# A fused attention and FFN block on one core: units of attention B in pairs, with another order of ACT, PE, DVE and POOL

## The reference, cut to what matters

```python
x = x + attn_a(layernorm(x))   # 16 heads of 64; q softmax over channels, k softmax over tokens,
                               # context = q^T k, out = context v, then w_out and b_out
x = x + ffn(layernorm(x))      # RWKV: token shift by mu_r, mu_k; sigmoid(xr W_r) * (relu(xk W_k)^2 W_v)
x = x + attn_b(layernorm(x))   # 16 heads of 8, rope on q and k,
                               # softmax(q k^T / sqrt(8)) v, then W_O
x = x + ffn(layernorm(x))      # the same weights
```

## Time and profile before

| | us |
|---|---|
| three runs | 1045.62, 1050.62, 1050.64; median 1050.62 |
| the profiled execution, whole | 1045.19 |
| its span (first to last instruction) | 1043.4 |
| busy: PE / ACT / DVE / POOL | 951.9 / 735.1 / 610.4 / 507.7 |
| share of the span | 91% / 70% / 58% / 49% |
| mean granted TensorE clock | 0.971 |
| chain that ended last | PE 72%, ACT 14%, DVE 6%, issue 3% |

### The profile page before, as it was taken

The page is one execution under the profiler, slowest core; times in us unless marked ns, Lnnn a source line. Parts: engine busy times, 40 slices in busy tenths (PEclk is TensorE's granted clock), DMA queues, the critical chain, the costliest instruction groups (busy, mean ns, idle before and its releaser), DMA issues.

```text
span 1043.4 us, 21070 instructions
## 1 busy us (share of the span) xinstructions
PE 951.9 (91%) x8139; PEld 510.9 (49%) x8139; DVE 610.4 (58%) x1475; ACT 735.1 (70%) x772; POOL 507.7 (49%) x344
## 2 busy tenths in 40 slices
PE   5985889999999999999999999999999999597983
PEld 3874534545454555545454545545554544232322
DVE  5776446566573847556573847656574745655233
ACT  4554667877777777878777777878777776375860
POOL 3758163644727292744637382754637271425000
PEclk9999889999999999999999999999999999798995
DMA  6002222324132332324132232324132232223210
GB/s 174 8 31 90 68 97 69 125 58 133 46 107 87 88 97 83 120 72 127 48 113 78 83 97 82 117 71 132 46 110 69 72 111 72 81 66 101 74 34 15
DMA packets 68657, 87.44 MB, mean 84 GB/s; under 512 B 13633, under 2 KB 40130, under 8 KB 68546
## 3 DMA queue, kind: packets, MB, share of 16 engines
q1 hardware_dynamic: 68546, 85.96, 27.4%
HBM read 16.19 MB, written 20.97 MB: 36 GB/s over the span
## 4 chain that ended last, share of the span: by engine, by line
PE 72%; ACT 14%; DVE 6%; issue 3%; SPq 2%; POOL 2%; DMA 1%; ACTq 0%; DVEq 0%
PE PS L1537 19%; PE PS L1351 8%; ACT work L658 8%; PE PS L1493 7%; PE PS L1407 6%; PE PS L1353 6%; PE PS L1352 5%; PE PS L1346 4%; PE PS L1451 3%; ACT work L652 3%; PE PS L1445 3%; PE PS L1428 3%; PE PS L1458 3%; PE PS L1553 2%; PE PS L1420 2%
## 5 line engine op out<-in xcount | busy, mean ns | idle before, releaser
L658 ACT ACTIVATE work<-PS 128x2048 f32<-128x2048 f32 x224 | 420.8, 1878 | 43.0 <-PE PS L1493 39.0
L1537 PE MATMUL PS<-work,v 128*32 128x512 f32 x2048 | 276.1, 611 | 4.6 <-DVE U L1034 4.1
L652 ACT ACTIVATE work<-PS 128x512 f32<-128x512 f32 x256 | 152.3, 598 | 145.1 <-PE PS L1353 142.9
L426 POOL TENSOR_TENSOR rs<-ve,half_neg 128x4 f32<-128x4 f32 x64 | 65.4, 1022 | 358.7 <-DVE ve L878 358.7
L439 POOL TENSOR_TENSOR work<-work,q_rcp 128x1024 f32<-128x1024 f32 x64 | 121.9, 1904 | 122.0 <-DVE q_rcp L930 122.0
L1493 PE MATMUL PS<-q_st,k_st 32*128 32x512 f32 x896 | 114.5, 501 | 19.6 <-DMA q_st<-qk_lo 10.1
L1351 PE MATMUL PS<-wqk,h1h 128*128 128x512 f32 x256 | 123.7, 483 | 2.6 <-issue 2.6
L1352 PE MATMUL PS<-wqk,h1h 128*128 128x512 f32 x256 | 101.9, 398 | 0.0
L1353 PE MATMUL PS<-wqk,h1l 128*128 128x512 f32 x256 | 101.7, 397 | 0.0
L1493 PEld LDWEIGHTS PS<-q_st,k_st 32*128 32x128 f32 x896 | 43.3, 183 | 108.2 <-issue 76.6
L1351 PEld LDWEIGHTS PS<-wqk,h1h 128*128 128x128 f32 x256 | 48.6, 190 | 86.9 <-ACT work L652 31.0
(11 more groups left out here) (159 smaller groups left out, 1611.0 us busy)
## 6 DMA issues: line engine op xcount, KB each, us to landing
qkv_scratch<-qkv_sb SPq DMA_DIRECT2D x16, 768.0 KB, 4.9
rot<-qkv_sb SPq DMA_DIRECT2D x32, 256.0 KB, 3.0
k_st<-qk_hi SPq DMA_DIRECT2D x128, 64.0 KB, 2.1
k_st<-qk_lo SPq DMA_DIRECT2D x128, 64.0 KB, 2.1
q_st<-qk_hi SPq DMA_DIRECT2D x128, 64.0 KB, 2.1
q_st<-qk_lo SPq DMA_DIRECT2D x128, 64.0 KB, 2.1
parted<-U SPq DMA_DIRECT2D x52, 128.0 KB, 2.9
xa<-in_attn_a_x SPq DMA_DIRECT2D x16, 256.0 KB, 2.9
```

The costliest lines, as they stand in the source:

```text
L426: pool.tensor_tensor(rs[:, :], ve[:, :], half_neg[:, :], ALU.pow).then_inc(rstd[n].sem, 1)
L652: act.activation((EQ, EK)[r // 2][c % 2][:, (r % 2) * 512:(r % 2) * 512 + 512], PS[:, bank, :], ACT.Exp)\
L658: act.activation(probs[n % 2], PS[:, 0:4, :], ACT.Exp).then_inc(z["s_exp"].sem, 1)
L1537: mm = pe.matmul(PS[32 * h:32 * h + 32, 6, :], v_flat[p][:, kc, at:at + 32], probs[n % 2][:, h, :], start=(n % 8 == 0), stop=(n % 8 == 7), ...
```

## The change

- **Three probs buffers.** `work_b` is new; `exp_scores(n)` waits for the product with v of unit `n - 3` instead of `n - 2`. `qk_rot` and `r_sb` go to make room.
- **Pairs.** The 16 units become 8 pairs `k`. ACT: `exp_scores(2k)`, `exp_half(2k - 1)`, `exp_scores(2k + 1)`, `exp_half(2k)`; half 15 falls into the next iteration. PE: `scores(2k)`, both `weigh_values` of the pair before, `scores(2k + 1)`, a small piece, `proj_half(2k)`, a small piece, `proj_half(2k + 1)`.
- **Bank 7** takes all of the small pieces in turn that were spread over banks 4 and 7. `r_copy` and `gates_copied` go; `gates` reads PSUM.
- **ACT gives to DVE** `m_copy`, `h1_copy`, two of the three `p_copy`, and the scaling by mu (`scale_mu` on ACT becomes `scale_and_mix` on DVE).
- **`context_narrow`** makes the context in tiles of 32 columns: 32 products instead of 16 in the code (64 for 32 in the trace, where each float32 product is two).
- **POOL, DVE and SP** get new orders. Rope stands right behind `q_hats(a, 0)` (before: behind `ln3_apply`); on DVE `ln1_norm` and the copy of `proj_b(2)` stand behind `q_sums(a, 0)`, and `ln_norm(1)` and `h1_copy` behind `q_sums(a, 1)`.
- Iteration 16 is a paired step without batch `a`; 17 to 19 drain as before, with the transposes of batch 0's attention B moved a little.

```diff
+        work_b = sb("work_b", [P, 2048])
+        probs = [w.rearrange("p (j n) -> p j n", j=4) for w in (work[:, 4096:6144], work[:, 6144:8192], work_b[:, :])]
```

The core of ACT's paired step:

```diff
+            def paired_step(i, p):
...
+                for k in range(8):
+                    exp_scores(z, b, 2 * k)
+                    if k == 0 and E:
+                        exp_half(s, 15, False)
+                    elif k > 0 and A:
+                        exp_half(a, 2 * k - 1, False)
+                    if E and k == 1:
...
+                        p_copy(l, 1)
+                    if k == 2:
+                        t_copy(s)
...
+                    if k == 5:
+                        hold(act, f1["x"], s - 1, 1)
+                        gates(f1, s, 7)
+                    if E and k == 7:
+                        hold(act, f2["x"], e - 1, 1)
+                        gates(f2, e, 7)
+                    exp_scores(z, b, 2 * k + 1)
+                    if A:
+                        exp_half(a, 2 * k, False)
```

PE's new context, and the core of its paired step:

```diff
+            def context_narrow(a, c):
+                hold(pe, q_hat, a, c + 1)
+                for t in range(PAIRS):
+                    for q in range(4):
+                        rows = slice(32 * q, 32 * q + 32)
+                        head = t * P + q // 2 * DA
+                        mm = pe.matmul(PS[rows, 5, t * DA:t * DA + DA], EK[c % 2][:, t * P + 32 * q:t * P + 32 * q + 32],
+                                       EQ[c % 2][:, head:head + DA], start=(c == 0 and t == 0), stop=(c == NC - 1),
+                                       tile_position=(0, 32 * q), skip_group_check=True)
...
+            def paired_step(i, p):
...
+                for k in range(8):
...
+                    scores(z, b, 2 * k)
...
+                    if k == 4 and A:
...
+                        context_narrow(a, 0)
...
+                    if k > 0:
+                        weigh_values(z, b, 2 * k - 2, 1 - p)
+                        weigh_values(z, b, 2 * k - 1, 1 - p)
+                    scores(z, b, 2 * k + 1)
...
+                    if k == 1 and E:
+                        proj_b(l, 2)
...
+                        wv_ctx_wout(s)
+                    if k == 3:
+                        if E:
+                            hold(pe, x1_ok, s)
+                            heads_out(z, e)
+                        if there(a + 1):
...
+                            head_T(a + 1, 7)
...
+                        proj_half(a, p, 2 * k, False)
...
+                    if k == 1:
+                        hold(pe, p_ev, l, 3 if E else 1)
+                        ctx_wout(s)
+                    if k == 2:
+                        attn_out(s, 1 - p)
...
+                    if k == 3:
+                        if there(a + 1):
+                            hold(pe, h1_sb, a + 1)
...
+                        ffn_T(f1, 1, s)
...
+                    if k == 7:
+                        if E:
+                            hold(pe, f2["x"], e, 1)
...
+                        h3_transposes(s)
+                    if A:
+                        proj_half(a, p, 2 * k + 1, False)
```

The places in DVE's paired step that follow the second and the fourth sum of q:

```diff
+                if A:
+                    sums_of(a, 1)
+                ln_norm(1, s, x1, hn1)
+                if there(a + 1):
+                    h1_copy(a + 1, 1 - p)
...
+                if A:
+                    sums_of(a, 3)
+                ln_norm(2, s, x2, h3)
+                if E:
+                    gate_v(f2, e)
```

726 lines of the change are left out of this document (348 added, 378 removed).

## The result

The changed kernel takes 1260.47 us (median of 4, 1259.57 to 1266.74), the kernel before on the same chip 1050.53: ratio 1.2025, 95% interval 1.1973 to 1.2077. The forecast was 1217 with its own bounds of 1180 and 1260, the range with the rivals 1070 to 1285. The profiled execution took 1259.57 us with a span of 1257.8, 214.4 more than the span before.

A forecast was written before the change was run, and what follows sets the result against it. PE bound the kernel, with about 1 us idle an iteration. Waits and clock raise 58.4 us to 73.75, +184 over 12 iterations, less 12 in iteration 16: span 1215, execution 1217; range 1180 to 1260, with rivals 1070 to 1285.

The forecast's parts named there:

- ACT's chain: Each pair's exponentials on ACT: no pair shorter than 6.52 us; 60 us an iteration; as the only bound 1052 us, 8%.
- nothing else late: Condition for ACT's order alone: the eight pairs take 60 us an iteration, 1.6 more than before.
- DVE behind the sum of q: Pairs 1, 3, 7: PE waits for DVE work behind a sum of q; 62.8 us an iteration, 4.4 more than before.
- POOL beside `ln1_norm`: Pair 1: `q_hats` and rope stretch `ln1_norm` to about 6.8 us; `ctx_wout` starts 6.4 us after PE got there.
- The rival of 18%: Rope or `q_hats` falls outside `ln_norm`, so only the sums bind: 62.8 us an iteration, 1087 us; chance 18%.
- The clock: After pair 1's wait PE runs at half clock: `ctx_wout` 2.4 us, the half 1.6, the next scores 0.36 more.
- The rival of 10%: Clock falls behind the waits in pairs 3 and 7 too: about 2.4 us each, 4.8 an iteration, 1275 us; chance 10%.
- Iteration 3 keeps its pattern: Iteration 3, ahead of the steady stretch, was taken as unchanged: 0 us, with the drain +-4.
- Iteration 16: As a paired step without projections it was to take 50 us instead of 62.5: -12 us.
- SP's order: SP's new DMA order, priced at nothing: stacked copies still issued at least one pair ahead of their scores.
- The narrow context: 64 products in four tiles: 1.08 us taken, as columns decide; bounds 1.08 and 2.16, 52 us at the other end.
- Faster by fewer changes between kinds of product: Rival on PE: each pair saves 0.26 us of changes, 3.1 an iteration with the idle us; 996 us, chance 12%.

The follow-up runs named there:

- e10: e9 with one DVE edit: `ln1_norm` right behind its stats, ahead of `c_norm`; 1063.59 us, ratio 1.0132.
- e8: e7 with `T_sb` copied by DVE behind `ln1_norm` instead of by ACT between pair 2's exponentials; 1107.81 us, ratio 1.0554.
- e4: e3 with the second and fourth sums of q moved behind `ln_norm` and the copy or gate after it; 1157.31 us, ratio 1.1039.
- e2: The changed kernel with only rope moved on POOL, back behind `ln3_apply`; 1257.75 us, ratio 1.2003.
- e1: The changed kernel with the third value product's copy to `qkv_sb` ahead of `ln1_norm` on DVE; 1248.42 us, ratio 1.191.
- e5: The changed kernel with 24 filler matmuls of 512 columns on PE ahead of `ctx_wout` in pair 1; 1257.24 us, ratio 1.1972.
- e6: The changed kernel with the earlier wide context (32 products in two tiles) in place of the narrow one; 1266.26 us, ratio 1.2075.
- e7: e4 with both `k_relu` ahead of the stats on DVE and POOL's second square ahead of the third rsqrt; 1124.06 us, ratio 1.0682.
- e9: e8 with rope behind `q_hats(0)` and `add_bias` on POOL, and the two looks at sums behind `add_x1` on DVE; 1118.14 us, ratio 1.0674.
- e3: The changed kernel with both the edit of e1 and rope moved behind `ln3_apply`; 1227.17 us, ratio 1.1711.

## Why the prediction was right, and where not

**ACT's chain.** Right as a mechanism, and in part by luck as a number. The forecast had 60 us an iteration with "nothing else late", and e10, with the long waits on DVE and POOL gone, has 60.1. But the forecast's 60 have `t_copy` on ACT, 8.3 us in pair 2, and e10 has it on DVE and 7.40 there; the other seven pairs are together 1.0 us longer than forecast. `t_copy` cost 0.96 of waiting in pair 2, and e8 gave 0.7 of it back. In iteration 3, pair 6 takes 6.49 (the minimum was put at 6.52). Of what PE idles more in e10 than before, 2.0 us an iteration are for ACT and 0.9 for DVE, and its busy time is 1.1 less: 1.7 us net, 21 in 12 iterations. With 3.4 us up to iteration 4 and 5.2 less in iteration 16 and the drain that makes the 19 us between the two spans (16 in the medians). So ACT's order is the larger part of why e10 is slower, not all of it; that its chain binds in the other pairs is read from these waits, and only `t_copy` was tested by an edit.

**DVE behind the sum of q.** Right: e4 takes the sums away from in front of `ln_norm`, and pairs 3 and 7 fall by 2.2 and 2.9 us. The forecast waits of 2.9 were 2.4. One small reading was off: sum and reciprocal take 1.50 from 515.62 to 517.12, not 1.47.

**POOL beside `ln1_norm`.** Right in place and size, 6.75 us; e2 and e10 show it from both sides (2.66 with `q_hats` alone beside it, and 1.12 with POOL free). The two causes are not separate: e1 alone brings 1.1 us an iteration, e2 alone 0.7, both 3.6, since each alone sends part of the wait elsewhere. The rival of 18%, that POOL doesn't bind, falls.

**The clock.** In pair 1 right (e5: 1.64 us there, forecast 1.76). The rival of 10%, that it falls behind pairs 3 and 7 too, came in part: pair 4 takes 8.24 on average and 7.45 at full clock, pair 7 in iterations 4 to 13 10.77 and 10.06; that is 1.5 us an iteration, not 4.8. In all, PE is busy 718.4 us in iterations 4 to 15 and 674.5 in e10, which does the same work at 1.00: by an estimate from these two, the clock costs 44 us of the 207 there; the rest is 176 us more idle time, less 13 by which PE's work itself is shorter (687.4 before).

**Mis-sized terms of the sum.** Against 1217 it is 43 us more. (1) Iterations 4 to 15: +22.3, by pairs 12 x 0.94 = 11.3 in pair 4 and 12 x 0.67 = 8.0 in pair 7, most of both the clock's (pair 7 waits 3.3 us in iterations 14 and 15 besides), and 12 x 1.07 = 12.8 in pair 6, where `k_relu` stands behind x2's stats, a wait that I had not looked for; less 10.2 in pair 1 (iteration 15 has no `ln1_norm` and takes 8.11), and small ones. So the terms miss in both directions, and that 1260 lies at the upper edge of the forecast's own bounds owes something to that. (2) Iteration 3: +13.5 where I took 0. "Iteration 3 keeps its pattern" was wrong. It is the first paired step; there rope stands behind the second `q_hats`, `ln_norm(1)` takes 6.74 us, and `ffn_T` waits 6.96: pair 3 takes 14.16 for 7.07. Pairs 1 and 7 are 3.1 and 4.4 longer. (3) Iteration 16 came to 51.8 (I took 50), but stood at 59.9 before and not 62.5, so the gain behind iteration 15 was 6.9 and not 12. (4) 0.9 stand ahead of iteration 3; the last us is rounding. SP's order, priced at nothing, cost nothing in iterations 4 to 15: no scores wait for a DMA there.

**The narrow context.** The trace of after settled it: 1.03 us at full clock, where I took 1.08 between 1.08 and 2.16. The Trainium skill (TensorEngine Tiling (Array Packing), Performance Considerations) has about 60 cycles a matmul, by which 64 would take an estimated 1.6 us; the row and e6 disagree, and the measurement decides: 64 products in four tiles take 16 ns each.

**Faster by fewer changes between kinds of product.** Not as a time: even e10, which keeps that order and has only short waits left, is 1.3% slower. PE's busy time did fall, by 1.1 us an iteration (57.3 to 56.2) where the rival had 2.1, and the waits on ACT take more than that. How much of the 1.1 is the order, and how much the narrow context and the other edits, no run separates.

## What to carry to other kernels

When an order is changed so that the bound engine has less slack, ask for every wait what stands in front of its producer on the other two engines, and go through each iteration that differs from the steady one. Small DVE instructions that take all their inputs from SBUF (scalings, sums of two tiles, moments) belong where POOL is idle: ahead of what releases POOL's next long instruction, not behind it (e10: 55 us of 1118). Taking one wait away tells little by itself, since the next late producer is often less than a us behind (e1, e2, e7, e9); compare the length of each stage and not the time alone.

## What the hardware showed

- A chain of short DVE instructions that read and write SBUF gets about one step for each POOL instruction beside it, however short its own steps: four of 0.34 us took 1.12 with POOL free (e10), 2.66 beside one POOL instruction (e2), 6.75 beside three in the changed kernel and 7.95 beside four (e1), in every iteration alike; a start 0.8 us ahead of the next POOL instruction changed nothing (e9). Held in this way were TENSOR_SCALAR, TENSOR_TENSOR and SCALAR_TENSOR_TENSOR with all of their inputs in SBUF. Not every DVE instruction is: beside POOL's work the stats (0.28 us each) and the sum of q (1.22) kept their time, RECIPROCAL (128x512) took 3.34 beside rope's third instruction at 583.72, and 3.35 on average in the kernel before, and those that read PSUM kept their time too (0.74 us at 490.40 in e4). The Trainium skill (SBUF — State Buffer, SBUF: two separate sides) has the shared pair of ports as a lock for a whole instruction; the trace agrees, and adds that in a train the two engines alternate.
- The clock's loss isn't tied to one wait, nor to its length. With pair 1's wait filled (e5), the waits of 2.4 us in pairs 3 and 7, which left the clock at 1.00 before in some iterations, were followed by a lower one in all of iterations 4 to 9 (0.85 to 0.94). In e3, where pair 1 has no wait, pair 3 waits just as long as in the changed kernel (2.5 us) and stays at 1.00 in all of iterations 4 to 14. Why, these runs don't settle.
